# Six packed buffers, stores 14 steps behind, and three stages written out without loops, in a four-layer graph network

## The reference

```python
h = jnp.maximum(_layernorm(x), 0.0)
msg = jnp.concatenate([h[src], edge_feats], -1) @ W1 + b1
msg_sum = segment_sum(msg, dst);  deg = segment_sum(ones, dst)
node_msg = msg_sum / jnp.maximum(deg, 1.0)[:, None]
out = node_msg + (node_msg @ W2 + b2)
x = x + jnp.where(out >= 0, out, RRELU_EVAL_SLOPE * out)
...
h = jnp.maximum(_layernorm(x), 0.0)
# layer 2: sparse attention over the edges, x + attn, batchnorm, feed forward, batchnorm
```

## Time and profile before

| | |
|---|---|
| median of 3 runs | 6019.27 us (6014.14 to 6030.68) |
| profiled execution, its own time | 6022.17 us |
| its span, first to last instruction | 6020.4 us |
| granted TensorE clock, mean | 0.809 |
| busy share PE / DVE / ACT / POOL | 63% / 66% / 34% / 50% |
| DMA engines, mean | 165 GB/s |

### The profile page before, as it was taken

How to read it: one execution, slowest core, us unless ns; L and a number is a source line. 1 busy time by engine, 2 the same in 40 slices (tenths; PEclk the granted TensorE clock), 3 DMA queues, 4 the chain that set the end, 5 groups by cost and what they waited for, 6 DMA issues and landing times. The chain is left out here.

```text
span 6020.4 us, 90405 instructions
## 1 busy us (share of the span) xinstructions
PE 3782.8 (63%) x16668; PEld 2549.2 (42%) x16668; DVE 3973.2 (66%) x12622; ACT 2020.3 (34%) x4450; POOL 2987.1 (50%) x2764
## 2 busy tenths in 40 slices
PE   0688884333489985559965556776500198988940
PEld 0466653333267764444444445555400043433410
DVE  8555555888388873654455556656578798888856
ACT  0444452333122221225556542222144433333310
POOL 0644442777677600000057768777700267777730
PEclk9788886555799997989977779888855599999975
DMA  6566665777455544877777767777578511111149
GB/s 226 147 160 159 156 159 152 230 221 211 121 127 145 142 157 153 255 241 229 229 230 234 226 187 135 133 127 133 94 256 271 177 32 38 43 46 47 48 156 377
DMA packets 986437, 994.99 MB, mean 165 GB/s; under 512 B 210641, under 2 KB 648417, under 8 KB 986163
## 3 DMA queue, kind: packets, MB, share of 16 engines
q1 hardware_dynamic: 676899, 628.12, 36.1%
q0 software_dynamic: 131904, 146.31, 12.7%
q10 hardware_dynamic: 177488, 218.95, 10.3%
HBM read 560.95 MB, written 466.16 MB: 171 GB/s over the span
## 5 line engine op out<-in xcount | busy, mean ns | idle before, releaser
L703 POOL DMA_INDIRECT at_first_table<-n_h,n_first_edge x784 | 792.6, 1011 | 1280.9 <-ACT n_h L271 924.5
L2489 PE MATMUL e_m<-e_by_rel,rel_w 128*128 128x512 f32 x1568 | 727.9, 619 | 0.0
L695 POOL DMA_INDIRECT e_xs<-x_table,e_idx x392 | 376.8, 961 | 514.1 <-POOLq L2379 395.0
L695 POOL DMA_INDIRECT e_x<-x,e_idx x392 | 376.9, 961 | 447.5 <-ACT e_h L271 241.0
L695 POOL DMA_INDIRECT e_hs<-h_table,e_idx x392 | 422.3, 1077 | 172.1 <-issue 108.1
L2403 DVE SCALAR_TENSOR_TENSOR e_by_rel<-e_y,e_part_t 128x512 f32<-128x512 f32 x784 | 476.5, 681 | 33.3 <-PE e_y L2504 27.7
L703 POOL DMA_INDIRECT rel_sum_table<-e_res,e_again x392 | 393.8, 1005 | 148.8 <-issue 125.5
L2489 PEld LDWEIGHTS e_m<-e_by_rel,rel_w 128*128 128x128 f32 x1568 | 306.1, 201 | 352.8 <-issue 352.8
L1008 PE MATMUL n_m<-n_mean,n_pick 128*128 128x129 f32 x784 | 203.4, 440 | 338.7 <-DVE n_pick L1073 323.0
L2481 PE MATMUL e_t<-ident,e_part 128*128 128x128 f32 x392 | 69.1, 304 | 550.7 <-ACT e_part L271 438.7
L711 POOL DMA_INDIRECT sum_table<-e_res,e_target x196 | 308.5, 1574 | 139.5 <-issue 58.9
(11 more groups left out here) (374 smaller groups left out, 10328.1 us busy)
## 6 DMA issues: line engine op xcount, KB each, us to landing
x_table<-n_x ACTq DMA_DIRECT2D x294, 256.0 KB
n_x<-x_table SPq DMA_DIRECT2D x294, 256.0 KB
e_hd<-at_first_table SPq DMA_DIRECT2D x196, 256.0 KB
mean_runs_table<-e_packed SPq DMA_DIRECT2D x196, 130.0 KB
n_mean<-mean_runs_table SPq DMA_DIRECT2D x392, 65.0 KB
at_first_table<-prep_zero ACTq DMA_DIRECT2D x1, 25088.0 KB
e_edge<-edge128T SPq DMA_DIRECT2D x98, 256.0 KB
e_keep<-col_tab_table SPq DMA_DIRECT2D x196, 128.0 KB
```

Source lines behind the costliest of these rows:

```text
L695: pool.indirect_dma_start(out=tile[:, t, :], out_offset=None, in_=table, in_offset=bass.IndirectOffsetOnAxis(ap=idx[:, col + t:col + t + 1 ...
L703: pool.indirect_dma_start(out=table, out_offset=bass.IndirectOffsetOnAxis(ap=idx[:, t:t + 1], axis=0), in_=tile[:, t, :], in_offset=None, ...
L2489: ins = pe.matmul(flat(at(ps_m, u - 6)), k.rel_w[:, r, :], at(by_rel, u - 6)[:, r, :], start=(r == 0), stop=(r == RELS - 1))
```

## The change

The first edge stage gets six buffers of packed means in place of four. ACT packing step j then waits for the store of step j - 6 and not j - 4. SP's stores run 14 steps behind its loads, not 16. And every engine of this stage and of the two run-reading node stages is written out: `each_step` calls the step function for every i from Python, with no loop, so that there is no branch and every address and count is a constant (the rows read from the table of starts excepted). The other stages keep `run_steps`.

```diff
+def each_step(body, steps, lag):
+
+    for i in range(steps + lag):
+        body(i, i)
@@ mean_edges
-        packed, packed_ready = ph.made("packed", [P, TILES, RUN_COLS], 4)
+        packed, packed_ready = ph.made("packed", [P, TILES, RUN_COLS], 6)
@@ SP: place_half
-                             at(packed, u)[:, HALVES * h:HALVES * h + HALVES, :]).then_inc(placed, 16)
+                             at(packed, j)[:, HALVES * h:HALVES * h + HALVES, :]).then_inc(placed, 16)
@@ SP: body
-                w = i - 16
+                w = i - 14
-            run_steps(sp, body, S, 16, 20)
+            each_step(body, S, 14)
@@ POOL, DVE
-            run_steps(pool, body, S, 0)
+            each_step(body, S, 0)
-            run_steps(dve, body, S, 9, 16)
+            each_step(body, S, 9)
@@ ACT
-                    if begun(j - 4):
-                        act.wait_ge(placed, (j - 3) * HALVES * 16)
+                    if begun(j - 6):
+                        act.wait_ge(placed, (j - 5) * HALVES * 16)
-            run_steps(act, body, S, 11, 16)
+            each_step(body, S, 11)
@@ PE
-            run_steps(pe, body, S, 10, 16)
+            each_step(body, S, 10)
@@ mean_nodes: SP, POOL, PE, DVE, ACT; attention_nodes: SP, DVE, PE, ACT (nine times)
-            run_steps(...)
+            each_step(body, S, <the same lag>)
```

More of the change, by code:

```diff
@@ L981, in body @@
                     sp.dma_start(flat(at(x, u - 1)), rows_of(a["x"], j)).then_inc(at(x_in, u - 1), 16)
-            run_steps(sp, body, S, 1)
+            each_step(body, S, 1)
         @block.gpsimd
@@ L993, in body @@
                             at(scattered, u - 5))
-            run_steps(pool, body, S, 5, 12)
+            each_step(body, S, 5)
             for u in range(SLOTS):
@@ L1010, in body @@
                     ins.then_inc(mean_done, 1)
-            run_steps(pe, body, S, 1)
+            each_step(body, S, 1)
         @block.vector
@@ L1078, in body @@
                     norm.scale_of(dve, j, u - 3, h1_ready)
-            run_steps(dve, body, S, 4)
+            each_step(body, S, 4)
         @block.scalar
@@ L1099, in body @@
                     act.dma_start(rows_of(scratch["h1"], j), flat(at(h1, u - 5))).then_inc(at(h1_out, u - 5), 16)
-            run_steps(act, body, S, 5, 12)
+            each_step(body, S, 5)
             for u in range(SLOTS):
@@ L1661, in body @@
                     sp.dma_start(flat(at(h1, u)), rows_of(scratch["h1"], i)).then_inc(at(h1_in, u), 16)
-            run_steps(sp, body, S, 0)
+            each_step(body, S, 0)
         @block.vector
@@ L1710, in body @@
                     ins.then_inc(spread_done, 1)
-            run_steps(pe, body, S, 0)
+            each_step(body, S, 0)
         @block.scalar
```

## The result

The changed kernel takes 5969.65 us (5956.2 to 5976.73, 4 runs) beside 6021.39 us (6014.14 to 6030.68, 4 runs): ratio 0.9914, 95% interval 0.9897 to 0.9931. It is faster by 52 us, where 186 were forecast, and lies outside the range. The profiled execution took 5969.23 us (span 5967.4).

A forecast was written before the change was run, and what follows sets the result against it. It took a one-step circle, ACT's packing waiting for stores held behind `e_g`, to bound the first edge stage, with POOL and DVE limiting the first node stage: 6022.2 - 171 + 8 - 23 = 5836, median 5833 us (0.969), range 5770 to 5925.

The forecast's parts named there:

- I set the 3.7 us wait at zero.: First edge stage: ACT's wait each step for stores of packed means, 303.9 us in 600 us, goes away.
- I take 6.1 us a step: First edge stage: step falls from 7.955 to 6.1 us, saving 161 us over 87 steps; ends 5.7 and 6.9 us.
- steps 7 to 10: First edge stage before the change, packed ring still empty: 5.94 us a step, taken as nearest row to the changed stage.
- SP: 4.8 to 6.9 us a step.: First edge stage: two stores a step, each behind the one before, 2.41 to 3.45 us from one to the next.
- rows 3: First edge stage's profiled timeline before the change; cited against rival 1 for store to landing of at most 2.7 us.
- Rival 1: First edge stage: SP's pair of stores becomes the limit, 6.9 us a step, total 5902 us; chance 0.20.
- It is covered by about 1.5 us: First edge stage: SP's `e_idx` load behind its two stores still comes early enough for POOL's gather, by about 1.5 us.
- In the drain ... 10 us.: End of first edge stage: SP has two steps fewer to store after the last loads, saving 10 us.
- First node stage, +8.: First node stage written out: POOL stays the limit, held by faster DVE, 5.47 us a step, costing 8 us.
- Second run-reading stage, -23.: Second run-reading node stage written out: SP's step goes from 3.10 to 2.84 us, saving 23 us.
- rival 4: First edge stage: PE's clock drops, kernel slower; whole stage at the lower level costs +161 us, total 6155; chance 0.03.

The follow-up runs named there:

- 14 behind only: Kernel before with stores 14 steps behind in place of 16, its loops and four buffers kept: 6585.38 us, ratio 0.9896.
- unordered stores: Changed kernel with each half store sent to rows of its own, waiting for none before: 5799.16 us, ratio 0.9665; on slow chips 6458.58 (0.9698) and 6494.58 us.
- the fourth set: Runs on one chip: before 5999.79 us, changed 5927.66 (0.9893), changed with unordered stores 5799.16 (0.9665), changed with first node stage in loops 5905.13 (0.9851).

## Why the prediction was right or wrong, by its steps

**"I set the 3.7 us wait at zero."** Right: the 303.9 us of waiting for stores are gone, and what `e_packed` still waits is 7.6 us for PE. The lag alone does it; six buffers and the written-out stage weren't needed for that (14 behind only, ratio 0.9896, on a slow chip).

**"I take 6.1 us a step" (the failed step).** The stage went at 7.30 us, 6.99 on another chip. The nearest row, steps 7 to 10 at 5.94 us, had one feature that decided: the stores were not yet in it. The prediction said so, and counted them as bytes only. As bytes they are harmless: with unordered stores the same bytes went at 5.806 us a step. As a chain of two round trips they are the limit. 87 x (7.955 - 7.300) = 57 us were saved in place of 161.

**"SP: 4.8 to 6.9 us a step."** The bound was too low. The upper end took 3.45 us, one interval of the earlier trace rows, for both stores. The pair has 7.0 to 7.4 us in the changed kernel: 2.9 to 3.0 us for one store, 4.2 to 4.4 us for the one that stands behind 464 KB of loads (256, 64, 128 and 16 KB; the 580 KB of an expectation above is too much, since `e_keep` has two bytes a number). The 2.7 us from store to landing in rows 3 held because SP's wait for `e_g` had let its queue run down in the middle of the loads. In the kernel before, on the chip of the fourth set, SP waits in 500 us

```profile
SPq L773 <- PE e_g L921: 122.0, 64, 3.2
SPq L753 <- DMA mean_runs_table<-e_packed: 6.6, 18, 0.6
```

that is 1.9 us a step for `e_g` and hardly at all for a landing; in the changed kernel there the wait for `e_g` is 1.6 us in all, and those for landings are 94.3 and 21.1 us, 1.6 us a step. The interval over the loads fell from 4.71 to 2.87 us, and the next one grew from 3.02 to 4.19: of 1.84 us gained 1.17 were given back at once, since the store now stands behind loads that are still running. The trace's records of single packets on SP's queue show it (the stores' packets are those of 520 bytes; the same two traces, 300 to 800 us, means). When the second store is issued, 144 KB of the step's loads are unfinished before the change and 312 KB after; the last of them ends 1.73 and 2.32 us later, and the store's own last packet 2.17 and 3.20 us later. The first store of the changed kernel, with no load ahead of it, has its last packet done 1.60 us behind its issue. Rival 1 was the right mechanism, with its mark at lines 758 and 759, and its price of 6.9 us a step was 0.1 to 0.4 us too low.

**"It is covered by about 1.5 us" (`e_idx`).** Wrong, and it is how the chain reaches the engines: POOL's wait for `e_idx` was 152.7 us in 68 steps. With the load taken off SP the wait went to `e_edge`, so the cover of one load wasn't the cause, only the place.

**"In the drain ... 10 us."** Right by itself, and of no use: behind the last load (`e_row`, at 936.2 us before and 893.6 after) stood 17 stores and stand 13, and from there to the end of the stage it took 48.0 us before and takes 36.7. But that last load now comes 25.9 us behind the last `e_ht`, where it came 11.9 us behind it: SP, being the limit, is further behind the others when the loads end. From the last `e_ht` to the end it was 59.9 us and is 62.6.

**First node stage, +8.** The right mechanism, mis-sized: +18.5 (+13 on another chip), 1.391 us a scatter where 1.37 was forecast, and 100 long ones for 54. Loops put back took it away (1.337 us). Under which operations a scatter is held, the changed kernel's trace tells: all 100 that took over 1.1 us began inside `n_leaky` (73) or `n_pick` (27), which take both their inputs from SBUF, and none of the 51 that began inside `n_biased`, which has one input in PSUM (the memory that PE writes), or inside the statistics. (13 began near the end of `n_x`, also with two inputs in SBUF, and took at most 1.02 us.) In the edge stage 75 gathers began inside `e_res`, which has an input in PSUM too, and none took over 0.95 us; of 73 that began inside the scan 58 were held. For `n_pick` in the kernel before:

```profile
1495.69 0.69 DVE L1073 TENSOR_TENSOR n_pick<-place_row,local 128x512 f32<-128x512 f32 x1
1495.77 1.47 POOL L703 DMA_INDIRECT at_first_table<-n_h,n_first_edge  x1 [0.30 <-DVE n_first_edge L1059]
```

The rule cited from the Trainium skill ("SBUF — State Buffer", section "SBUF: two separate sides") is of operations in a two-port mode. The section also lets an operation with two inputs from SBUF contend with a GpSimd instruction that reads SBUF, and that is what the trace agrees with, in the counts above. That the cause is the lock of that section no run here shows by itself. On the slow chips the sign turns (657.5 written out, 707.7 in loops), so this is a finding of one kind of chip.

**Second run-reading stage, -23.** Right: -21.1, and 2.88 us a step for 2.84.

**PE's clock (rival 4).** It rose from 0.84 to 0.87, where above 0.9 was forecast, and it was not the limit: 0.98 with a step of 6.81 us, 0.93 with 5.81.

## What to carry to other kernels

When a row is taken from a stretch in which one part doesn't run yet, cost that part as a chain and not only as bytes: here two ordered stores a step ran at their round trips, 7.3 us, with the DMA engines 70% busy, and unordered ones at 5.8 us a step. Read a round trip from the steady state and for each position in the queue, since the store behind 464 KB of loads took 4.2 us and its neighbour 2.9. A wait in the middle of a queue's work also lets the queue run down, so taking it away can make what stands behind it slower: here two thirds of what it freed came back as a later landing.

## What the runs showed of the hardware that was not expected

**Chips differ by stage, not evenly.** Where the kernel before takes 6660 to 6720 us in place of 6000 to 6020, the excess is in the stages with scatters and gathers by POOL: looped first node stage 692 to 718 us for 557, third node stage 682 to 696 for 527, last edge stage (from its first load of `e_again`) 1204 to 1233 for 980 to 989, second edge stage 887 to 900 for 840; the feed forward (348) and the third edge stage (811 to 820, and 803 to 817) are the same. One and the same edit, writing the first node stage out, gives 641 to 658 us there, some 50 less than the loops, and 16 more on the chip of the fourth set. How the change as a whole does there was not measured.

**Standstills.** On the slow chips POOL's gathers in the first edge stage stood still for over 5.5 us 8 to 10 times with unordered stores and 23 times in each kernel with `e_idx` from ACT, 1 to 4 times in the four others; on the first kind never, in twelve traces. In one on a slow chip, with unordered stores, PE's last `e_c` of a step is recorded from 500.96 to 501.35, and ACT and DVE, which wait for it, go on together 5.3 us later:

```profile
500.96 0.39 PE L941 MATMUL e_c<-e_res,e_pick 128*128 128x130 f32 x2
...
506.69 0.39 ACT L857 ACTIVATE e_packed<-e_c 128x260 f32<-128x260 f32 x1 [7.19 <-remote]
506.77 1.01 DVE L826 TENSOR_SCALAR e_pick<-place_row,e_row 128x128 f32<-128x128 f32 x4 [6.41 <-remote]
```

The same kernel on the first kind of chip had a step of 5.806 us for 6.84 to 6.89. Why these signals come late, the trace doesn't show, and it stays open.
